# First batch of a 16-head attention part: rotation on VectorE, stacking of the queries' rows ahead of the keys' stores, and a later place for loads

## What is computed

```python
x = _layernorm(x + _L0_attn_ref(x, w_qkv, w_proj))
# in _L0_attn_ref, hd = 16, 16 heads:
qkv = x @ w_qkv
q = q * cos + _rotate_half(q) * sin
k = k * cos + _rotate_half(k) * sin
attn = softmax(einsum('bhqd,bhkd->bhqk', q, k) * hd ** -0.5)
out = einsum('bhqk,bhkd->bhqd', attn, v) ... @ w_proj
```

## Time and profile before

| what | value |
|---|---|
| median of 3 runs | 2366.89 us |
| profiled execution, its own time | 2371.28 us |
| its span (first to last instruction) | 2369.4 us |
| mean granted clock of PE | 0.963 of full speed |
| busy share of the span: PE, DVE, ACT, POOL | 94%, 71%, 65%, 56% |
| first `amax` matmul of batch 0 starts at | 54.14 us |

### The profile page before, as it was taken

How to read it: one execution, slowest core, us unless ns; L and a number is a source line. 1 busy time by engine, 2 the same in 40 slices (tenths; PEclk the granted TensorE clock), 3 DMA queues, 4 the chain that set the end, 5 groups by cost and what they waited for, 6 DMA issues and landing times. The chain is left out here.

```text
span 2369.4 us, 44936 instructions
## 1 busy us (share of the span) xinstructions
PE 2217.9 (94%) x14760; PEld 1568.6 (66%) x14760; DVE 1682.7 (71%) x3272; ACT 1532.7 (65%) x3482; POOL 1330.7 (56%) x1392
## 2 busy tenths in 40 slices
PE   2899999899999999879999999999799999998997
PEld 1544444444444444368888888788688888887886
DVE  1677788677877888377777777565477787775674
ACT  1277787777878887646777676454367776674442
POOL 3334566433334443677777765464377767664675
PEclk7699999999999999899999999999999999999999
DMA  8657666756666666211000000100100000001111
GB/s 182 98 106 138 127 128 130 155 137 136 141 136 145 164 155 147 91 40 37 2 1 1 2 1 10 59 12 3 38 2 1 2 1 1 1 4 34 50 53 41
DMA packets 92261, 160.80 MB, mean 68 GB/s; under 512 B 15832, under 2 KB 35016, under 8 KB 92040
## 3 DMA queue, kind: packets, MB, share of 16 engines
q1 hardware_dynamic: 89480, 149.54, 28.4%
q0 software_dynamic: 2560, 8.39, 1.0%
HBM read 93.28 MB, written 59.24 MB: 64 GB/s over the span
## 5 line engine op out<-in xcount | busy, mean ns | idle before, releaser
L943 DVE TENSOR_REDUCE MX<-PS 128x1 f32<-128x512 f32 x1024 | 642.3, 682 | 200.0 <-PE PS L533 189.6
L783 ACT ACTIVATE PT<-PS 128x512 f32<-128x512 f32 x1024 | 546.5, 600 | 141.2 <-PE PS L550 139.4
L533 PE MATMUL PS<-KS,QS 48*128 48x512 f32 x1024 | 357.4, 454 | 56.4 <-DMA KS<-hs 45.9
L550 PE MATMUL PS<-QS,KS 50*128 50x512 f32 x1024 | 387.7, 460 | 6.6 <-ACT PT L783 6.3
L550 PEld LDWEIGHTS PS<-QS,KS 50*128 50x128 f32 x1024 | 165.8, 189 | 273.9 <-issue 215.6
L566 PE MATMUL PS<-PT,VP 128*17 128x512 f32 x2048 | 277.7, 615 | 2.9 <-ACT OT L790 2.8
L636 PE MATMUL PS<-kT,qT 128*128 128x256 f32 (+1 forms) x1536 | 253.4, 306 | 0.0
L533 PEld LDWEIGHTS PS<-KS,QS 48*128 48x128 f32 x1024 | 171.6, 192 | 121.3 <-issue 59.8
L1314 POOL TENSOR_TENSOR PB<-PB,RC 128x512 f32<-128x512 f32 (+1 forms) x256 | 235.1, 935 | 11.5 <-DVE RC L1068 11.5
L855 ACT ACTIVATE PB<-PS,NMf 128x256 f32<-128x256 f32 (+1 forms) x512 | 223.7, 450 | 24.5 <-DVE NMf L1059 22.5
L1294 POOL TENSOR_TENSOR RI<-RI,mhalf 128x8 f32<-128x8 f32 x128 | 213.9, 1671 | 10.7
(11 more groups left out here) (182 smaller groups left out, 5297.7 us busy)
## 6 DMA issues: line engine op xcount, KB each, us to landing
hs<-HL SPq DMA_DIRECT2D x64, 512.0 KB, 3.8
QS<-hs SPq DMA_DIRECT2D x192, 128.0 KB, 6.1
KS<-hs SPq DMA_DIRECT2D x192, 128.0 KB, 8.4
od<-OT SPq DMA_DIRECT2D x64, 256.0 KB, 5.5
OC<-od SPq DMA_DIRECT2D x32, 256.0 KB
cst<-rs SPq DMA_DIRECT2D x32, 256.0 KB
X<-x SPq DMA_DIRECT2D x8, 512.0 KB, 8.7
tab<-ctxT SPq DMA_DIRECT2D x8, 512.0 KB, 7.2
```

The costliest lines, as they stand in the source:

```text
L533: pe.matmul(PS[:, bank, :], QS[rows, s, h // 2, qt * P:(qt + 1) * P], KS[rows, s, h // 2, :], start=True, stop=True).then_inc(fills("amax" ...
L550: pe.matmul(PS[:, bank, :], KS[rows, s, pair, kt * P:(kt + 1) * P], QS[rows, s, pair, :], start=True, stop=True).then_inc(fills("score", v ...
L783: act.activation(PT[:, kt % 2, 2 * i + half], PS[:, TURNS["score", vb, g, kt, half, i][0], :], ACT.Exp).then_inc(drains("score", vb, g, kt ...
L943: dve.tensor_reduce(MX[:, vb % 2, h // 8, qt, c:c + 1], PS[:, TURNS["amax", vb, h, qt][0], :], AX, ALU.max).then_inc(drains("amax", vb, h, ...
```

## The change

Batch 0 gets an order of its own, `FIRST_BATCH`, and leaves the table for what lies ahead of step 0 and for `stack`. Its `mix`, `mix_sum` and `heads_lo` are now done by DVE; POOL does them for batches 1 to 7 as before (POOL's first `mix` of batch 1 waits for the four `heads_lo` of batch 0). `stack` of batch 0 becomes four pieces `stack_first(0, qk, half)`, each of six loads, and each waits only for the two stores of its own qk. Of the weights only q and k are split ahead of the transposes' parts; v and o are loaded behind `tab` and the ones and split at the end of `FIRST_BATCH`. X of sequence 1 is loaded at the start, X of sequence 2 and the biases behind the stack loads of batch 0, X of sequences 3 to 7 in slot 12 of steps 0 to 4.

```diff
+FIRST_BATCH = (
+    ("tr", 0), ("tr_hi", 0), ("tr", 1), ("tr_hi", 1), ("tr_lo", 0), ("tr_lo", 1), ("rope", 0, 0), ("rope_out", 0, 0), ("mix", 0, 0),
+    ("rope", 0, 1), ("rope_out", 0, 1), ("mix", 0, 1), ("rope", 1, 0), ("rope_out", 1, 0), ("mix_sum", 0, 0), ("heads_hi", 0, 0), ("mix_sum", 0, 1),
+    ("rope", 1, 1), ("rope_out", 1, 1), ("heads_hi", 0, 1), ("heads_lo", 0, 0), ("heads_lo", 0, 1), ("heads_out", 0, 0), ("heads_out", 0, 1),
+    ("mix", 1, 0), ("mix", 1, 1), ("mix_sum", 1, 0), ("heads_hi", 1, 0), ("mix_sum", 1, 1), ("heads_hi", 1, 1), ("heads_lo", 1, 0), ("heads_lo", 1, 1),
+    ("stack_first", 0, 0), ("heads_out", 1, 0), ("heads_out", 1, 1), ("stack_first", 1, 0), ("stack_first", 0, 1), ("stack_first", 1, 1),
+)
...
+    out += [(s[0], 0) + s[1:] for s in FIRST_BATCH] + [("split_w", 0, 2), ("split_w", 0, 3)]
+    out += [("load_x", 2), ("load_bias",)]
...
                 vb = step - k
+                if vb == 0 and (k < 0 or kind == "stack"):
+                    continue
...
+        if 0 <= step and step + 3 < NB:
+            at[12].append(("load_x", step + 3))
...
-    out = [("begin",)] + [("load_w", 0, j) for j in range(4)] + [("loads",)] + [("split_w", 0, j) for j in range(4)] + head_stages() + list(LAST_BATCH[-3, 0]) + window_first(0)
+    out = [("begin",), ("load_w", 0, 0), ("load_w", 0, 1), ("loads",), ("load_w", 0, 2), ("load_w", 0, 3), ("load_x", 1), ("split_w", 0, 0), ("split_w", 0, 1)] + head_stages() + list(LAST_BATCH[-3, 0]) + window_first(0)
...
# in vector(dve):
+            def mix(vb, qk, tile):
+                if vb == 0:
+                    T = TM[:, qk]
+                    if qk == 0 and tile == 0:
+                        dve.wait_ge(sem["tab"], 16)
+                    dve.wait_ge(*drained("rope", vb, qk, tile))
+                    for k in range(2):
+                        source, table = T[:, 2 * tile], tab[:, (1 + tile + k) % 2]
+                        dve.tensor_tensor(T[:, 2 * tile + 1 - k], source, table, ALU.mult).then_inc(sem["turned"], 1)
...
# in gpsimd(pool), and likewise in mix_sum and heads_lo:
             def mix(vb, qk, tile):
+                if vb == 0:
+                    return
                 T = TM[:, qk]
-                if vb == 0 and qk == 0 and tile == 0:
-                    pool.wait_ge(sem["tab"], 16)
+                if vb == 1 and qk == 0 and tile == 0:
+                    pool.wait_ge(sem["heads_lo"], 4)
...
# in sync(sp):
+            def stack_first(vb, qk, half):
+                for tile in range(2):
+                    heads_written(sp, vb, qk, tile)
+                stack_rows(0, qk, half)
```

More of the change, by code:

```diff
@@ L938, in tr_lo, with mix_sum, heads_lo @@
                 dve.tensor_tensor(xT[:, half, 1], PS[:, bank, :], f(xT[:, half, 0]), ALU.subtract).then_inc(drains("tr", vb, half), 1)
+            def mix(vb, qk, tile):
[7 more added lines that the diff above has]
+                        dve.tensor_tensor(T[:, 2 * tile + 1 - k], source, table, ALU.mult).then_inc(sem["turned"], 1)
+            def mix_sum(vb, qk, tile):
+                if vb == 0:
+                    T = TM[:, qk]
+                    dve.wait_ge(sem["turned"], 4 * qk + 4)
+                    if tile == 0:
+                        dve.tensor_tensor(T[:, 0], T[:, 0], T[:, 2], ALU.subtract).then_inc(sem["rope_sum"], 1)
+                    else:
+                        dve.tensor_tensor(T[:, 1], T[:, 1], T[:, 3], ALU.add).then_inc(sem["rope_sum"], 1)
+            def heads_lo(vb, qk, tile):
+                if vb == 0:
+                    n = n_split(vb, qk, tile)
+                    hb = (n - 1) % 3
+                    dve.wait_ge(sem["heads_hi"], n)
+                    dve.tensor_tensor(HL[:, hb, 1], TM[:, qk, tile], f(HL[:, hb, 0]), ALU.subtract).then_inc(sem["heads_lo"], 1)
             def amax(vb, h, qt):
@@ L1174, in fnorm @@
                 m.then_inc(sem["fnormed"], 1)
-            does = dict(begin=begin, split_w=split_w, tr_lo=tr_lo, amax=amax, fold=fold, inv=inv, res=res, stats=stats, norm_last=norm_last, window_consts=window_consts, rot=rotations, split_qkv=split_qkv, wzero=wzero,
+            does = dict(begin=begin, split_w=split_w, tr_lo=tr_lo, mix=mix, mix_sum=mix_sum, heads_lo=heads_lo, amax=amax, fold=fold, inv=inv, res=res, stats=stats, norm_last=norm_last, window_consts=window_consts, rot=rotations, split_qkv=split_qkv, wzero=wzero,
                         wtrl=wtrl, wrot=wrot, wsum=wsum, wadd=wadd, wqkl=wqkl, wmax=wmax, wrecip=wrecip, wol=wol, wres=wres, mzero=mzero, mstat=mstat,
@@ L1386, in loads, with load_bias @@
                         sp.dma_start(f(KS[r:r + 2, s]), f(NM[:])).then_inc(sem["ones_k"], 16)
-                for b in range(1, NB):
-                    load_x(b)
+            def load_bias():
                 sp.dma_start(bq[:], t["xbqk"]).then_inc(sem["bq"], 16)
@@ L1409, in heads_out, with stack_rows @@
                 sp.dma_start(v, f(HL[:, hb])).then_inc(sem[f"heads{hb}"], 16)
+            def stack_first(vb, qk, half):
+                for tile in range(2):
+                    heads_written(sp, vb, qk, tile)
+                stack_rows(0, qk, half)
+            def stack_rows(s, qk, half):
+                T, parts = ((QS, (0, 0, 1)), (KS, (0, 1, 0)))[qk]
+                v = t["hs"][s, qk, half * P:(half + 1) * P].rearrange("(n r d) a t -> r a d n t", r=2, d=16)
+                for k, a in enumerate(parts):
+                    for r in range(2):
+                        row = 64 * r + 16 * k
+                        sp.dma_start(f(T[row:row + 16, s, 4 * half:4 * half + 4]), v[r, a]).then_inc(sem[f"stack{s}{half}"], 16)
             def stack(vb, half):
@@ L1417, in stack @@
                     sp.wait_ge(*filled("score", vb - 2, 2 * half + 1, 3, 1, 1))
[L1418 to L1423, removed]
+                for qk in range(2):
+                    stack_rows(s, qk, half)
             def negmax_out(vb, half):
```

5 lines of the change are left out of this document (4 added, 1 removed).

## The result

| | before | changed |
|---|---|---|
| median of 20 runs each, us | 2368.32 (2357.81 to 2386.72) | 2355.13 (2346.75 to 2369.79) |
| profiled execution: its own time, span | 2371.28, 2369.4 | 2355.35, 2353.1 |
| mean granted clock of PE | 0.963 | 0.966 |
| first `rope` matmul starts at | 11.93 | 8.96 |
| last `heads_lo` ends at | 35.40 | 24.60 |

The ratio of the two is 0.9945, with a 95% interval from 0.9925 to 0.9966: 13.0 us less, between 8.0 and 17.8. Single runs of one kernel spread over more than 20 us, far more than the three runs ahead of the prediction (3.7) had shown.

A forecast was written before the change was run, and what follows sets the result against it. PE's wait for the KS loads was taken as the bound; earlier weights, DVE rotation and the DRAM trip bring the first amax from 54.14 to 44.1, so 2366.9 - 10.0 = 2356.9 us, range 2352.0 to 2362.0 (8 in 10).

The forecast's parts named there:

- What bounds the kernel: Whole run: PE's 33.7 us wait for KS delays the first amax to 54.14; bringing it forward moves the end equally.
- Weights: Start, up to the first rope: four casts before xT instead of eight, so rope starts at 8.84, 3.1 us earlier.
- Rotation on DVE: Making queries and keys: last heads_lo ends at 24.95 against 35.40; 7.4 of the 10.4 us come from the engine.
- Stores and stack loads: DRAM trip: keys' stores queue behind QS loads, 1.8 us each, landing at 35.7; first amax at 44.1, 10.0 earlier.
- So the early QS loads win little: DRAM trip: without the early QS loads amax would start at 43.6, since the queue gives back the overlap's saving.
- Moving them avoids a clash rather than saving time: Start: later loads of X and biases avoid a clash with the first store at 18.6; no saving counted.
- The rate: Stack loads: 128 KB in 1.04 us, 126 GB/s; at the skill's 104 GB/s the total would be 2359.6 us.
- X bites in the steps: Steps 1 to 4: loads of X delay stores and reach PE; 6.0 us saved, 2360.9 us; chance 0.20.
- The stores do not stand behind the loads: DRAM trip: keys' stores land at 31.0, undelayed by QS loads; 14.7 us saved, 2352.2 us; chance 0.08.
- Nothing measurable left: Steps: four loads of X cost their whole time, 11.1 us together, giving 2368.0 us; chance 0.07.
- PE's clock, slower: Step 1: PE regains its upper clock level later; 40 us longer at the lower gives 2377 us; chance 0.05.
- The pace at the start: Start: PE's quicker pace might stay at 17.6 instead of moving to 14.5, delaying the second heads_hi by 1.7 us.

The follow-up runs named there:

- the second profile: The changed kernel run again with no edit: median 2354.49 us of 12 runs, ratio 0.9947 to the kernel before; first amax at 41.74.
- the run with interleaving: Changed kernel with both keys' stores behind the first of six loads into QS instead of the sixth: median 2351.23 us of 12 runs, ratio 0.9937.
- The run without the split: Changed kernel with batch 0's stack loads in one piece behind all four stores: 2361.57 us in a single run; first amax at 44.39.
- the kernel before with DVE alone: Kernel before with only batch 0's mix, mix_sum and heads_lo moved to DVE: 2371.35 us beside 2369.90, one run each; first amax at 47.39.
- 100 matmuls: Changed kernel with 100 matmuls of unread result on PE between the last rope and first amax: 2355.62 us in a single run.
- 112: Changed kernel with 112 matmuls of unread result on PE before the first amax: 2347.90 us beside 2364.67 of the kernel before, one run each.

## Why the prediction was right

The forecast was 10.0 us less, the measurement 13.0 with an interval from 8.0 to 17.8, by the mechanism that was named: the long wait of PE ends earlier, and all that follows comes earlier by as much.

- **What bounds the kernel**: right. The start gave 11.8 of it, and the distance to batch 6 did not change beyond what repeats of one kernel differ by.
- **Weights**: first `rope` at 8.96, forecast 8.84; 2.97 where 3.1 stood. The step was right for this pair of profiles, but it took a late landing of w_o in one execution for a property of the kernel. With that weight in time it is 0.9 to 2.1. (The addends, 6.8 and 2.01, give 8.81 and not 8.84.)
- **Rotation on DVE**: the last `heads_lo` ended at 24.60, forecast 24.95. The chain from rows of before, instruction by instruction, was off by 0.35 us over 16. Part of that is luck: it took PE's change of pace 5.7 us behind the restart for granted, and it came at 6.1 here and at 3.9 in the second profile, whose last `heads_lo` ended at 24.16 though its `rope` began 0.23 later. As a saving *on the path* it isn't 7.4: added alone it gave 6.0, and undone in the changed kernel it cost 3.0 to 3.9.
- **Stores and stack loads**: this is the term that was mis-sized. From the last `heads_lo` to `amax` it was 17.7, forecast 19.2. "1.8 each" for a store behind the loads was worked out from the 4.0 of a lone store less "about 2" of latency, which no row gives and which would leave 2.0; measured, two stores landed 2.3 after the load ahead of them, 1.15 each, and 6.2 to 6.9 after issue instead of 8 to 9. That is 1.3 of the 1.8 us by which `amax` beat the forecast of 44.1. That the stores stand behind the loads was right (the earlier trace rows had shown it); the run with interleaving moved them and got part of the delay back. The Trainium skill (DMA: Bandwidth & Descriptors, Queues, rings and completion order) says that each DMA engine consumes its descriptors in ring order; the trace agrees, with 6.2 to 6.9 us against 4.0 for a store alone.
- **A better price stood in the same rows**: the store of the earlier trace rows landed 0.6 after the load ahead of it, and it was half as large as one of `heads_out`, 256 KB against 512, as the kernel before's page says in the line below. Scaled by its bytes that makes 1.2 for 512 KB, near the measured 1.15.

```profile
od<-OT SPq DMA_DIRECT2D x64, 256.0 KB, 5.5
```

- **"So the early QS loads win little"**: wrong in size. The run without the split puts them at about 2 us, by the same error.
- **"Moving them avoids a clash rather than saving time"** (X and the biases): right about the clash, but it stood outside the sum, and its size was not worked out. Against the kernel before, in which the loads of X were hidden, it is indeed no saving. Within the change it is worth 3.1 to 3.9 us, since the rotation on DVE makes them visible.
- **The rate**: 128 to 130 GB/s in the changed kernel's first profile, as in the earlier trace rows, and 137 to 140 in its second. By the 104 GB/s that the Trainium skill (SBUF — State Buffer, Door 1) lists for 16 partitions the first `amax` would have come near 47, by the prediction's estimate; it came at 42.33. The interleaved kernel's profile reached 180 GB/s, so neither the row is a limit, nor the listed figure, beyond which, as the prediction has it, more loads in flight would not help.

The rivals. *X bites in the steps*: false; ACT never waited for a store there, between 100 and 420. *The stores do not stand behind the loads*: false, by their landing. *Nothing measurable left*: false. *PE's clock, slower*: false. The low stretch moved along with the work: it stood from about 83 to 117 before and from about 66 to 104 in the changed kernel, and in all 14 profiles it ended 58 to 64 us behind the first `amax`. The pace at the start changed at 15.07 and not at 17.6. The Trainium skill (TensorE: Matmul & The Clock Gate, Part 1) calls the throttled state the default which activity releases. The start agrees as far as it goes: PE's pace rose after its restart in every profile, 5.7 us behind it before and 6.1 now, but 3.9 in the changed kernel's second profile and under 3 in the kernel before with DVE alone. The stretch from 66 on does not: PE was busy 32.82 of 38 us there and the clock was low, as this window of the changed kernel shows.

```profile
66.00:104.00 38.00, 32.82 (x81) 18.23 (x81) 29.57 (x49) 5.74 (x11) 11.61 (x13) 0.51 0.81 130
```

That the sum came so close is in part luck. The weights were charged with 1.0 to 2.2 us more than they are worth when none lands late, and the two stores with 1.3 us more than they cost; the two errors have opposite signs. And the profile of before, from which 54.14 was read, was one in which w_o landed late.

The range of 10 us was narrow for what it rested on, a spread of 3.7 us over three runs: 20 runs of the changed kernel spread over 23.

## What to carry to other kernels

Where a prologue ends in a trip through DRAM, look at what stands in the one DMA queue ahead of each store that somebody waits for: bulk loads that cost nothing beside a slow engine cost 3 to 4 us once that engine is fast, and six stack loads ahead of two stores cost the stores 2 to 3. Then ask how little the first dependent instruction really needs: half-sized first loads brought the first scores 3.4 to 4.5 us forward, and together with the interleaving 7.7 to 8.4. That such a gain at the start arrives whole at the end is not shown here. Parts of such a change do not add up; take each away from the finished kernel, and also add it alone to the old one, and judge by moments of the trace where single runs scatter more than the effect.

## What the runs showed of the hardware that was not expected

- Stack loads of 16 partitions and 128 KB ran with full engines at 128 to 130 GB/s in the changed kernel's first profile, at 137 to 140 in its second and at 177 to 182 in the interleaved kernel's. One and the same kernel has more than one level; the cause is open.
- The first loads of 64 KB into KS landed 2.2 to 2.3 us after issue, at a DMA share of about 0.5, where the first six of 128 KB took 3.0 to 5.6 at a share above 1.
- Behind a gap of 2.41 us at the end of 100 matmuls the next work ran at the lower level; behind a gap of 0.21 us at the end of 112 it ran at the upper one (one profile each).
- The same kernel needed 50.1 or 52.4 us from the first `amax` to the first exponential, by one more dip of the granted clock.
